# T4 of the first chunk and a half sum of Wh made while Wh arrives, with the parts of Wx spread anew over steps 2 to 6

## The reference

```python
xW = jnp.einsum('ntd,dg->ntg', x, Wx) + b      # Wx is 512 x 2048
def step(carry, xw_t):
    prev_h, prev_c = carry
    a = xw_t + prev_h @ Wh                     # Wh is 512 x 2048
    i, f, o = sigmoid(a[:, :Hd]), sigmoid(a[:, Hd:2*Hd]), sigmoid(a[:, 2*Hd:3*Hd])
    g = jnp.tanh(a[:, 3 * Hd:])
    next_c = f * prev_c + i * g
    next_h = o * jnp.tanh(next_c)
    return ((next_h, next_c), next_h)
return x + swapaxes(scan(step, (h0, 0), swapaxes(xW, 0, 1)), 0, 1)
```

## Time and profile before

| | us |
|---|---|
| median of 3 runs | 2542.74 (2542.69 to 2542.77) |
| the profiled execution's own time | 2543.45 |
| its span, first to last instruction | 2541.4 |
| TensorE busy | 2525.8 (99%) |
| VectorE busy | 1938.7 (76%) |
| ScalarE busy | 1554.5 (61%) |
| GpSimd busy | 160.8 (6%) |

### The profile page before, as it was taken

The page is one execution under the profiler, slowest core; times in us unless marked ns, Lnnn a source line. Parts: engine busy times, 40 slices in busy tenths (PEclk is TensorE's granted clock), DMA queues, the critical chain, the costliest instruction groups (busy, mean ns, idle before and its releaser), DMA issues.

```text
span 2541.4 us, 161390 instructions
## 1 busy us (share of the span) xinstructions
PE 2525.8 (99%) x67268; PEld 1801.8 (71%) x67268; DVE 1938.7 (76%) x8091; ACT 1554.5 (61%) x5895; POOL 160.8 (6%) x264
## 2 busy tenths in 40 slices
PE   9999999999999999999999999999999999999998
PEld 3677777777777777777777777777777777777775
DVE  7777777777777777777777777777777777777776
ACT  8666666666666666666666666666666666666664
POOL 1000000000000000000000000000000000000000
PEclk9999999999999999999999999999999999999999
DMA  7111111111112111111121111111111121111111
GB/s 238 43 37 37 41 45 37 37 41 45 37 37 41 45 37 37 41 45 37 37 41 45 37 37 41 45 37 37 41 45 37 37 42 45 37 37 43 43 33 35
DMA packets 58364, 114.24 MB, mean 45 GB/s; under 512 B 6496, under 2 KB 7136, under 8 KB 57312
## 3 DMA queue, kind: packets, MB, share of 16 engines
q0 software_dynamic: 19008, 35.53, 9.9%
q1 hardware_dynamic: 39248, 78.30, 9.1%
q10 hardware_dynamic: 80, 0.03, 0.0%
HBM read 79.23 MB, written 33.55 MB: 44 GB/s over the span
## 4 chain that ended last, share of the span: by engine, by line
PE 98%; DVE 1%; DMA 1%; ACT 0%; SPq 0%; issue 0%; DVEq 0%; ACTq 0%
PE Z L389 72%; PE run L389 19%; PE extra L389 6%; DMA h_T<-in_h_cols 1%; DVE wx_lo L932 0%; ACT tanh_c L644 0%; DVE h_hi L994 0%; SPq L309 0%; DVE gc L1011 0%; DVE igfc L1005 0%; ACT act L633 0%; ACT wx_hi L658 0%; DVE gc L1020 0%; DVE igfc L1007 0%; DVE hT_hi L999 0%
## 5 line engine op out<-in xcount | busy, mean ns | idle before, releaser
L389 PE MATMUL Z<-wh_hi,hT_hi 128*32 128x512 f16 x8176 | 795.9, 379 | 7.0 <-DVE hT_hi L999 6.9
L389 PE MATMUL Z<-wh_lo,hT_hi 128*32 128x512 f16 x8176 | 796.0, 379 | 0.0
L633 ACT ACTIVATE act<-Z 128x128 f32<-128x128 f32 x1024 | 287.2, 281 | 569.7 <-PE Z L389 569.7
L389 PE MATMUL Z<-wh_hi,hT_lo 128*32 128x512 f16 x8176 | 529.8, 379 | 0.0
L644 ACT ACTIVATE tanh_c<-gc 128x64 f32<-128x64 f32 x1024 | 262.8, 257 | 311.3 <-DVE gc L1020 248.7
L389 PE MATMUL run<-wx_hi,x_hi 128*32 128x256 f16 x6048 | 427.3, 273 | 1.2 <-DVE x_lo L799 1.2
L389 PE MATMUL Z<-wx_hi,x_hi 128*32 128x256 f16 x6048 | 427.4, 273 | 0.2 <-DVE wx_lo L932 0.2
L389 PE MATMUL Z<-wx_lo,x_hi 128*32 128x256 f16 x6048 | 427.3, 273 | 0.0
L389 PE MATMUL Z<-wx_hi,x_lo 128*32 128x256 f16 x6048 | 427.3, 273 | 0.0
L389 PE MATMUL run<-wx_lo,x_hi 128*32 128x256 f16 x6048 | 427.3, 273 | 0.0
L389 PE MATMUL run<-wx_hi,x_lo 128*32 128x256 f16 x6048 | 427.3, 273 | 0.0
(11 more groups left out here) (121 smaller groups left out, 3923.3 us busy)
## 6 DMA issues: line engine op xcount, KB each, us to landing
y<-in_x_rows POOLq DMA_DIRECT2D x127, 256.0 KB, 4.0
out_y<-y SPq DMA_DIRECT2D x127, 256.0 KB, 2.0
x_T<-in_x_cols SPq DMA_DIRECT2D x126, 256.0 KB, 2.7
wx_raw<-in_Wx SPq DMA_DIRECT2D x4, 1024.0 KB, 12.8
wh_raw<-in_Wh SPq DMA_DIRECT2D x4, 1024.0 KB, 13.5
t<-in_Wx SPq DMA_DIRECT2D x3, 512.0 KB, 18.5
t<-in_Wx POOLq DMA_DIRECT2D x3, 512.0 KB, 5.8
x_raw<-in_x_cols SPq DMA_DIRECT2D x2, 256.0 KB, 6.2
```

Of the source, the lines that this page charges most:

```text
L389: return nc.tensor.matmul(out, lhsT, rhs, start=False, stop=last, skip_group_check=True)
L633: nc.scalar.activation(half_gates(act, a)[:, 0:2], half_gates(Z[s], a)[:, 0:2], ACT.Sigmoid, scale=scale).then_inc(gates_done, 1)
```

## The change

T4 of chunk 0 gets a place of its own, the second half of t1, and is made right after the cuts of T2; it no longer waits for the raw products or the cut of B21. T1 of chunk 1, which had that place, is loaded into the raw place of B21's chunk 0 instead, and its load waits on SyncE for the raw products, for T4 and for the low cut of B21. The half sum of chunk 2 of Wh moves from ScalarE to VectorE, and ScalarE's high cut of T3 of chunk 0 moves ahead of its last two sums. The high cut of T1 of chunk 1 moves from step 3 to step 4, that of B22 from step 4 to step 5. The low cut of T4 of chunk 0 moves from step 2 to step 6, ahead of that of chunk 1. `W_ORDER` and `CUT` are the same.

```diff
--- before.py
+++ after.py
@@ -98,7 +98,7 @@
 
 
 
-        wh_sum = sb("wh_sum", [P, NCH + 1])
+        wh_sum = sb("wh_sum", [P, NCH + 2])
         wx_sum = sb("wx_sum", [P, 2, 4])
         wmax = sb("wmax", [P, 2])
         wmax_all = sb("wmax_all", [P, 2])
@@ -264,6 +264,10 @@
                 return t1[:, 0]
             if cp == 1 and k == W_NAMED["T4"]:
                 return t3[:, 0]
+            if cp == 0 and k == W_NAMED["T4"]:
+                return t1[:, 1]
+            if cp == 1 and k == W_NAMED["T1"]:
+                return w_block(1, 0)[:, 0]
             return (w_block(0, 0), w_block(1, 0), w_block(1, 1), w_block(1, 0), t1, w_block(0, 1), t3)[k][:, cp]
 
 
@@ -352,8 +356,11 @@
             load_x(2, 0)
             load_x(3, 1)
             sp.dma_start(t3[:, 1], Wx[3][:, HG:]).then_inc(t3_loaded, 16)
-            sp.dma_start(t1[:, 1], Wx[1][:, HG:]).then_inc(t1_loaded, 16)
             sp.dma_start(bias_d[:, :], bias_rows[:, HW:]).then_inc(bias_d_loaded, 16)
+            sp.wait_ge(raw_done, 2)
+            sp.wait_ge(t4_made, 1)
+            sp.wait_ge(wx_lo_cut, CUT[W_NAMED["B21"], 0] + 1)
+            sp.dma_start(w_form(W_NAMED["T1"], 1), Wx[1][:, HG:]).then_inc(t1_loaded, 16)
             sp.wait_ge(wx_lo_cut, CUT[W_NAMED["T3"], 0] + 1)
             sp.dma_start(t3[:, 0], Wx[3][:, 0:HG]).then_inc(t4_loaded, 16)
             sp.wait_ge(wx_lo_cut, CUT[W_NAMED["T1"], 0] + 1)
@@ -689,9 +696,10 @@
             sum_of_wh(0, G)
             cut_wx_hi(0, "T2")
             sum_of_wh(1, G)
-            sum_of_wh(2, G)
+            cut_wx_hi(0, "T3")
+            sum_of_wh(2, HG)
             sum_of_wh(3, HG)
-            cut_wx_hi(0, "T3", "B22", "T4")
+            cut_wx_hi(0, "B22", "T4")
             sc.wait_ge(w_scale_done, 1)
             cut_wh_hi(0)
             sc.wait_ge(z_done, 1)
@@ -718,13 +726,14 @@
                     cut_wx_hi(1, "T2")
                     scale_raw(5)
                 if s == 3:
-                    cut_wx_hi(1, "B21", "T1")
+                    cut_wx_hi(1, "B21")
                     scale_raw(6)
 
             def last_cuts(s):
                 if s == 0:
-                    cut_wx_hi(1, "T3")
                     scale_raw(7)
+                    cut_wx_hi(1, "T1", "T3")
+                if s == 1:
                     cut_wx_hi(1, "B22")
                 if s == 2:
                     cut_wx_hi(1, "T4")
@@ -872,18 +881,18 @@
                 nc.vector.tensor_reduce(wx_sum[:, cp, 2:3], wx_raw[:, ch, HG:], AX.X, ALU.add,
                                         apply_absolute_value=True).then_inc(wx_summed_2, 1)
 
-            def sum_of_last_wh():
-                v.wait_ge(wh_loaded[3], 16)
-                nc.vector.tensor_reduce(wh_sum[:, 4:5], wh_raw[:, 3, HG:], AX.X, ALU.add,
+            def sum_of_half_wh(ch):
+                v.wait_ge(wh_loaded[ch], 16)
+                nc.vector.tensor_reduce(wh_sum[:, ch + 2:ch + 3], wh_raw[:, ch, HG:], AX.X, ALU.add,
                                         apply_absolute_value=True).then_inc(wh_summed_2, 1)
 
             def largest_weight(k):
 
                 if k == 0:
                     v.wait_ge(wh_summed, NCH)
-                    v.wait_ge(wh_summed_2, 1)
-
-                    nc.vector.tensor_tensor(wh_sum[:, 3:4], wh_sum[:, 3:4], wh_sum[:, 4:5], ALU.add).then_inc(wh_sums_joined, 1)
+                    v.wait_ge(wh_summed_2, 2)
+
+                    nc.vector.tensor_tensor(wh_sum[:, 2:4], wh_sum[:, 2:4], wh_sum[:, 4:6], ALU.add).then_inc(wh_sums_joined, 1)
                     v.wait_ge(wh_sums_joined, 1)
                 else:
                     v.wait_ge(row_max_done, 2)
@@ -920,8 +929,6 @@
 
             def make_t4():
                 v.wait_ge(t2_made, 1)
-                v.wait_ge(raw_done, 2)
-                v.wait_ge(wx_lo_cut, CUT[W_NAMED["B21"], 0] + 1)
                 nc.vector.tensor_tensor(w_form(W_NAMED["T4"], 0), w_block(1, 0)[:, 0], w_form(W_NAMED["T2"], 0),
                                         ALU.add).then_inc(t4_made, 1)
 
@@ -973,8 +980,9 @@
                 cut_wx_lo(0, "B11")
                 make_t2()
                 cut_wx_lo(0, "B21", "T1", "T2")
-                sum_of_last_wh()
                 make_t4()
+                sum_of_half_wh(2)
+                sum_of_half_wh(3)
                 largest_weight(0)
                 cut_wx_lo(0, "T3")
                 weight_scale(0)
@@ -1076,7 +1084,6 @@
                         scale_tables()
                         scale_block(2, 0)
                     if first(n) and s == 2:
-                        cut_wx_lo(0, "T4")
                         cut_wx_lo(1, "B11")
                     if first(n) and s == 3:
                         cut_wx_lo(1, "T2")
@@ -1086,6 +1093,7 @@
                         if s == 1:
                             cut_wx_lo(1, "T3", "B22")
                         if s == 2:
+                            cut_wx_lo(0, "T4")
                             cut_wx_lo(1, "T4")
                     if s == 3 and within(n + 3, NB):
                         field_of_sum(n + 3, 1 - r)
@@ -1143,7 +1151,7 @@
 
             share_wmax(0)
             add_w(t3[:, 1], t3_loaded, Wx[1][:, HG:], t3_added)
-            add_w(t1[:, 1], t1_loaded, Wx[1][:, 0:HG], t1_added)
+            add_w(w_form(W_NAMED["T1"], 1), t1_loaded, Wx[1][:, 0:HG], t1_added)
             add_w(bias_d[:, :], bias_d_loaded, bias_rows[:, 0:HW], bias_d_done)
             add_w(t1[:, 0], t2_loaded, Wx[1][:, 0:HG], t2_added)
             share_wmax(1)
```

## The result

| | us |
|---|---|
| before, median of 20 runs | 2542.74 (2542.61 to 2543.47) |
| changed, median of 20 runs | 2547.37 (2546.61 to 2548.95) |
| ratio | 1.0018, 95% interval 1.0012 to 1.0024 |
| the changed kernel's profiled execution, own time and span | 2548.46 and 2546.4 |

The change makes the kernel 4.6 us slower, 0.18%, and its runs spread over 2.3 us where those of before lie within 0.9. Two executions in what follows, one of before (4303.16 us) and one of the kernel with counts that fit (5556.39 us), stood far off at a mean granted clock of 0.58 and 0.45, and are left out of every comparison. In the changed kernel the lines of before are moved by 7 to 9: 389 is 396, 932 is 939, 1005 is 1013, 799 is 808.

The account below looks back on a forecast made before the run. TensorE was taken to bound the kernel, with only the time before step 8 open to change. Head and loads 0, added wait +1.7 net of earlier gains, clock +1.7, taken as 3.6: 2542.74 + 3.6 = 2546.3 us, range 2544.3 to 2547.6.

Parts of the forecast that it names:

- What bounds the kernel: TensorE, busy 99% of the span; only what happens before step 8 starts at 78.18 us can change the time.
- The head: Before step 0: first high cut of Wh some 1.13 us earlier, taken up by ScalarE's wait for Z; value 0.
- the loads: T1 of chunk 1 loaded behind SyncE's waits: taken as 0, at worst 0.3 us for GpSimd's queue, hidden by slack.
- Steps 2 to 5: Moved cuts bring cell(3) 0.76 us and cell(4) 0.99 us earlier; 1.2 to 1.6 us gained up to cell(6).
- The added wait: Step 6: B22 of chunk 1 waits for the 13th low cut, TensorE idles 4.2 us, step 8 starts 1.7 us later.
- The clock: Behind step 6's idling TensorE falls to half clock: again +1.7 us, bounds 0 and 3.4.
- a second slow stretch: Rival: TensorE's clock stays at half for another stretch behind 77 us; +5.3 us, 2548.0; chance 0.10.
- The rival in which the wait isn't felt: Step 6: another count holds, cell(7) has both T4 cuts ahead, step 8 near 77.8; -0.4 us, 2542.3; chance 0.06.
- The sum: Added wait and clock, 1.7 + 1.7: 3.4 us without the fall at 60 us, 3.8 with it; 3.6 taken.
- the main case: Wait felt in step 6 and clock falls behind it: median 2546.3, own bounds 2545.8 to 2547.3; chance 0.68.

Follow-up runs that it names:

- counts that fit: The changed kernel with products waiting for the number each low cut really has (T4 of chunk 0 the 13th): 2542.98 us, ratio 1.0000.
- the head alone: The changed kernel with every cut of Wx in the step it had before, so only the head and loads are new: 2542.78 us, ratio 0.9999.
- once more: The changed kernel as it is, the last of its two further profiled executions: 2547.24 us.
- the filled kernels: Groups of zero matmuls in the two waits behind step 3: on the kernel before, 2542.82 us; on the changed kernel with T4's low cut in the head, 2541.81.
- T4's cut alone: The kernel before with only the low cut of T4 of chunk 0 moved from step 2 to step 6: 2547.82 us, ratio 1.0020.
- the wait filled: The changed kernel with 36 groups of four zero matmuls ahead of B22's wait in step 6: 2545.12 us, ratio 1.0008.

## Why the prediction was right, and where its sizes were off

- **What bounds the kernel.** Right: the spans differ by 5.0 us and the starts of step 8 by 5.05.
- **The head, value 0, and the loads, value 0.** Right, shown by the head alone (2542.78). The gain at the cut of Wh was 0.92 us where I had put 1.13: VectorE's cut of T2 came later in this execution, so that T4 began at 18.66 and the two half sums behind it ended only at 22.3. It made no difference, for ScalarE's wait for Z took it.
- **Steps 2 to 5.** Right nearly to the hundredth: cell(3) at 51.89 (51.84 forecast), cell(4) at 57.41 (57.42), the recurrent parts at 53.53 and 59.06 (53.50 and 59.08). In the first execution, with the fall in step 5, cell(5) was at 63.88 (63.66) and cell(6) at 69.92 (69.70); without it, "once more", they were at 63.25 (63.27) and 69.29 (69.31). What I had given too much weight to is T1's cut leaving step 3: with T4's cut moved alone, cell(4) is already at 57.62.
- **The added wait.** Right in place, cause and length: a wait for the 13th cut, 4.00 us (4.2 forecast), and shown from both sides, by counts that fit and by the one moved line. What was mis-sized is its term of the sum, +1.7 us (2.1 with the fall in step 5): measured 2.3. I summed against the one profiled execution, which had a fall in step 5, and carried the result over to the median as though the median run had one. That it stood 0.71 us above the median was on the page, and the fall explains about 0.6 of this. Against the faster base the gain of steps 2 to 5 is smaller and the loss larger by 0.6 us.
- **The clock.** Right in kind, +1.7 us in size; measured 2.25 on the median, and 2.2 to 2.8 in the profiled executions. The step that failed is the length that I took over from the fall before. There TensorE was busy through all of the slow stretch, and it lasted 3.4 us; here it began in the wait and lasted 6.8 us. My rival of a second slow stretch (+5.3 us, 2548.0) is thus half true: the stretch is as long as two, but a part lies in the wait, where it costs nothing. And the sentence that two gaps of hardly over 1 us brought the first fall was one execution's word; the filled kernels bear it out for about a quarter of the executions.
- **The rival in which the wait isn't felt** is the kernel with counts that fit. Its cell(7) did have both cuts of T4 ahead of it, as written (76.55), but step 8 came at 78.12 and the time was 2542.98, against 77.8 and 2542.3: the same base again.
- **The sum.** 3.6 forecast, 4.6 measured: the wait 2.3 us where the 3.6 holds 1.9 (the middle of 1.7 and 2.1), the clock 2.25 where it holds 1.7. The upper bound of the main case was also added up wrongly: 2542.74 + 3.8 + 0.4 is 2546.9 and not 2547.3, so 2547.37 lies 0.4 us above what the main case allowed, and within the range only because this reached up to 2547.6. The mechanism was forecast; that the number came inside is in part the width of the range.

The Trainium skill, "TensorE: Matmul & The Clock Gate", section "Why this matters for your kernels", warns of long idle gaps between bursts of matmuls, and the trace agrees for the wait of 4.0 us: in it the clock fell in all three profiled executions of the changed kernel and in that of T4's cut alone, and it stayed at 1.00 where the wait was filled. For the two waits behind step 3 no such plain rule holds: after 1.17 and 1.04 us the clock fell in the execution of before and after 1.17 and 1.03 or 1.16 and 1.03 it did not in those of the head alone and of T4's cut alone; after 1.10 and about 0.81 it fell in three of six.

## What to carry to other kernels

Where a semaphore counts pieces of work, the order of the pieces is part of every wait: who moves one piece moves the meaning of all numbers behind it, so the numbers are to be made from the order in which the work is really issued. It can go wrong the other way too: in the changed kernel the product T4 of chunk 0 waits for 7 although its cut is the 13th, and only B22's wait for 13, which TensorE meets first, keeps it from reading a cut that isn't made. A gain of slack that ends in another wait is worth nothing by itself, but it is a place for work that costs elsewhere: with counts that fit, T4's low cut costs some 0.9 us in step 6 (2542.98 against 2542.03, less than the interval of the runs but borne out by the starts of step 8, 78.12 and 76.66, less 0.6 for the fall in the first) and nothing in the slack that the change had made in the head. A profiled execution that stands off the median may hold an event that the median run does not; look for it before you sum against it.

## What the runs showed of the hardware

- TensorE's slow stretches lasted about 3.4 us in step 5 (before, 60.2 to 63.6; changed, 59.4 to 62.8; the wait filled, 59.4 to 62.8; counts that fit, 58.8 to 62.2), and about 6.8 us in step 6, in four executions of two kernels. In step 6 TensorE had stood idle for 1.1 to 2.8 us when the clock fell and stayed idle for 1.2 to 2.9 more; in step 5 it was at work throughout, but for 0.04 us in the counts that fit. That this idle time is what makes the second kind longer is argued, not shown.
- Behind the same code the fall began at 73.1, 71.8 and 71.2 us in three executions; this alone spreads the times by 0.6 us, and the fall in step 5, which comes in some executions only, adds 0.6.
- Matmuls of zeros into a bank that nobody else used at the time kept the clock at full speed through a wait of 4 us. They cost nothing that the trace can tell: B22's product starts at 74.39, 1.29 us behind the start of VectorE's cut (73.10), as in the changed kernel (74.29 and 72.99).
